# A graph network's edge loop: PE makes the next group's pair counts between its two sums, and DVE takes them at the start of the turn

## What is computed

```
def _prop_once(node_states, f_idx, t_idx, edge_features, w1, b1, w2, b2, w3, b3):
    from_states = node_states[f_idx]
    to_states = node_states[t_idx]
    edge_inputs = jnp.concatenate([from_states, to_states, edge_features], axis=1)
    edge_states = _mlp(edge_inputs, w1, b1, w2, b2, w3, b3)
    return jax.ops.segment_sum(edge_states, t_idx, num_segments=node_states.shape[0])
agg = _prop_once(node_states, from_idx, to_idx, edge_features, ...)
agg = agg + _prop_once(node_states, to_idx, from_idx, edge_features, ...)
...
S = jax.ops.segment_sum(X[src], dst, num_segments=n)     # second layer, three times
```

## Time and profile before

| | us |
|---|---|
| median of 3 runs | 2401.57 |
| lowest, highest | 2397.04, 2402.34 |
| the profiled execution, its own time | 2405.81 |
| its span, from the first to the last instruction | 2403.9 |
| first sum of the first turn, of the last turn | 67.0, 1907.8 |
| PE matmuls busy | 2278.5 (95%) |
| DVE busy | 1761.2 (73%) |
| ACT busy | 1230.7 (51%) |
| POOL busy | 1143.2 (48%) |

### The profile page before, as it was taken

One profiled execution on the slowest core, in us unless ns is written; L12 is line 12 of the kernel. 1 busy time (PEld: TensorE's weight loads), 2 busy tenths in 40 slices (PEclk: granted clock), 3 DMA queues, 4 the chain that ended last, 5 costly groups with the idle time before them and its releaser, 6 DMA issues. The chain is left out here.

```text
span 2403.9 us, 39417 instructions
## 1 busy us (share of the span) xinstructions
PE 2278.5 (95%) x12547; PEld 1876.2 (78%) x12547; DVE 1761.2 (73%) x4056; ACT 1230.7 (51%) x2106; POOL 1143.2 (48%) x846
## 2 busy tenths in 40 slices
PE   4999999999999999999999999999999879799997
PEld 3888888888888888888888888888888645588886
DVE  7888888888888888888888888888887557602114
ACT  4556556656656656556666566565665413211112
POOL 2556555656566666566566565665665300000000
PEclk9999999999999999999999999999999979899998
DMA  4356556446555445555535555544555450395873
GB/s 161 80 106 131 98 94 109 87 80 110 98 94 111 90 78 109 95 97 108 96 77 106 94 110 97 94 95 87 103 103 94 59 218 1 118 385 229 337 286 142
DMA packets 232338, 292.57 MB, mean 122 GB/s; under 512 B 126016, under 2 KB 189862, under 8 KB 223800
## 3 DMA queue, kind: packets, MB, share of 16 engines
q1 hardware_dynamic: 158756, 237.04, 36.0%
q0 software_dynamic: 73216, 54.58, 16.9%
q10 hardware_dynamic: 272, 0.05, 0.0%
HBM read 218.51 MB, written 73.08 MB: 121 GB/s over the span
## 5 line engine op out<-in xcount | busy, mean ns | idle before, releaser
L470 POOL DMA_INDIRECT sums<-outb,target x416 | 671.1, 1613 | 625.0 <-ACT outb L640 421.6
L463 POOL DMA_INDIRECT xg<-in_x,gidx x416 | 467.4, 1123 | 158.8 <-issue 140.9
L1237 PEld LDWEIGHTS ebank<-w3t,h 128*128 128x128 f32 x3328 | 387.4, 192 | 8.3 <-issue 0.3
L1237 PE MATMUL ebank<-w3t,h 128*128 128x128 f32 x3328 | 388.2, 275 | 0.2 <-ACT h L622 0.2
L1225 PE MATMUL ebank<-h1h,w2h 128*128 128x512 f32 x832 | 365.0, 439 | 5.1 <-DVE h1l L849 3.3
L622 ACT ACTIVATE h<-ebank,b2c 128x512 f32<-128x512 f32 x416 | 286.6, 689 | 116.2 <-issue 81.9
L608 ACT ACTIVATE h1h<-hpre 128x512 fp32r<-128x512 f32 x416 | 257.9, 628 | 154.6 <-DVE hpre L845 115.7
L1225 PE MATMUL ebank<-h1h,w2l 128*128 128x512 f32 x832 | 328.9, 395 | 0.0
L1225 PE MATMUL ebank<-h1l,w2h 128*128 128x512 f32 x832 | 326.3, 392 | 0.0
L849 DVE SCALAR_TENSOR_TENSOR h1l<-hpre,h1h 128x512 fp32r<-128x512 f32 x416 | 270.9, 691 | 17.2 <-ACT h1h L608 13.6
L845 DVE TENSOR_TENSOR hpre<-pb,ebank 128x512 f32<-128x512 f32 x416 | 265.1, 677 | 2.3 <-PE ebank L1211 2.2
(11 more groups left out here) (266 smaller groups left out, 3800.6 us busy)
## 6 DMA issues: line engine op xcount, KB each, us to landing
ring<-adj SPq DMA_DIRECT2D x54, 1568.0 KB, 8.4
rowb<-along SPq DMA_DIRECT2D x104, 512.0 KB
adj<-band SPq DMA_DIRECT2D x25, 1500.0 KB
ef<-in_edge_attr SPq DMA_DIRECT2D x103, 256.0 KB
stay<-adj SPq DMA_DIRECT2D x6, 1568.0 KB, 14.4
xg<-in_x,gidx POOLq DMA_INDIRECT x416
sums<-outb,target POOLq DMA_INDIRECT x416
sums<-band SPq DMA_DIRECT2D x2, 1664.0 KB
```

The costliest lines, as they stand in the source:

```text
L463: pool.indirect_dma_start(out=to, out_offset=None, in_=a["x"], in_offset=bass.IndirectOffsetOnAxis(ap=ids, axis=0)).then_inc(s_x[par], 16)
L470: pool.indirect_dma_start(out=tables[k % 2], out_offset=bass.IndirectOffsetOnAxis(ap=target[par][:, 1, k:k + 1], axis=0), in_=outb[par][:, ...
L1237: last = nc.tensor.matmul(bank[6 + way][:, t * P:(t + 1) * P], h2[:, way, k, t * P:(t + 1) * P], w3t[:, k, :], start=not bias and k == 0, ...
```

## The change

On PE, `pairs_of(g)` is no longer made between `turn_sd(g + 1)` and `second(g, 1)`. `total(g)` now makes `pairs_of(g + 1)` between the first sum and the second. In it a wait is added, for all four `hpre` of that group (`s_hp`), since `bank[4]` and `bank[5]` are free only then. Group 0 has its pair counts where they were.

On DVE, from turn 1 on, `count_pairs(g, 0)` is the first thing in the turn, then comes `nodes(g + 1)`, then `count_pairs(g, 1)`, and only then `compare`, `places` and `sums`. `lower_parts` now follows `sums` directly. No instruction of the computation is added or taken away.

```
-                    if ahead:
-                        nodes(g + 1, 1 - par, early=early == 2)
-                        compare(g + 1, 1 - par, turns + par)
-                    places(g, par, early=early > 0)
-                    if ahead:
-                        sums(g + 1)
                     if begin:
+                        nodes(1, 1, early=True)
+                        compare(1, 1, 0)
+                        places(0, 0, early=True)
+                        sums(1)
                         pair_keys()
                         pair_hot(0)
                         lower_parts(1)
                         dve.wait_ge(s_band, 2)
                         dve.wait_ge(s_ztab, 2 * 16)
-                    if fresh is not None:
-                        dve.wait_ge(s_fresh, fresh)
-                    count_pairs(g, 0)
-                    count_pairs(g, 1)
+                        count_pairs(0, 0)
+                        count_pairs(0, 1)
+                    else:
+                        if fresh is not None:
+                            dve.wait_ge(s_fresh, fresh)
+                        count_pairs(g, 0)
+                        if ahead:
+                            nodes(g + 1, 1 - par)
+                        count_pairs(g, 1)
+                        if ahead:
+                            compare(g + 1, 1 - par, turns + par)
+                        places(g, par, early=early > 0)
+                        if ahead:
+                            sums(g + 1)
...
                 def pairs_of(g):
 
                     pe.wait_ge(s_ah, g + 1)
+                    pe.wait_ge(s_hp, g * 4 + 4)
...
-                def total(g, par):
+                def total(g, par, ahead):
...
                     last.then_inc(s_sum, 1)
+                    if ahead:
+                        pairs_of(g + 1)
                     pe.wait_ge(s_es, g * 2 + 2)
...
                     if begin:
                         pair_keys()
-                    else:
-                        pairs_of(g)
                     second(g, 1)
```

More of the change, by code:

```diff
@@ L1316, in turn @@
                     third(g)
-                    total(g, par)
+                    total(g, par, ahead)
                 def into_each():
```

## The result

The changed kernel takes 2518.02 us (median of 4 runs, 2516.35 to 2519.22) against 2400.62 us for the kernel before (4 runs): a ratio of 1.0483, 95% interval 1.0469 to 1.0497. It is 117 us slower. The prediction was 2511 us, in a range of 2470 to 2541.

What follows compares the result with a forecast made beforehand. PE, busy 95% of the span, was taken to bound the kernel, others close behind. Turns of 18.95 against 17.92 us add 105 us, wraps 5; 2401.6 + 110 gives about 2511 us, range 2470 to 2541.

Steps and rivals of the forecast that it cites:

- Pairs on PE: PE, between the two sums: the four pair matmuls cost 0.96 us, as in the old place; bounds 0.83 and 1.1.
- The second sum's wait: PE's second sum starts at t + 1.80, t being the first sum's start, so its wait for `es` is covered.
- The first count is hidden: DVE, start of turn: half 0's count ends at t + 2.95, before `into` at t + 2.99, hidden by 0.04 us.
- The bubble: DVE, between `into` and second `outdeg`: 0.36 us idle for the slot read; chain to `sd` 1.05 us later in all.
- From `same` to the fourth block: DVE to ACT to PE: 3.05 us to `sd`, 2.40 to the fourth block at t + 9.84; PE waits 1.37 us.
- The rest of the turn: PE, behind the fourth block: 1.45 us to L1211, at t + 11.29, then 7.66 to the next first sum; 18.95 us.
- The sum: Edge loop: 1.03 us more in turns 1 to 102 is 105 us, with the wraps' 5, 110; about 2511.
- A: Rival: PE's fourth block doesn't wait, the turn is 17.54 us and some wraps, 24 to 30 us less, 2375; chance 0.06.

Runs made afterwards that it cites:

- e8: The kernel before with DVE's `pair_hot` moved behind `ways`; ratio 0.9920 to the kernel before.
- e10: e8 with DVE's target, the add that waits for the table's DMAs, also moved behind `sdl`; ratio 0.9908 to the kernel before.
- e3: The changed kernel with only DVE's second count moved back behind `sd`; 2409.67 us against 2409.09 for the kernel before, ratio 1.0008.
- e2: The changed kernel with ACT writing `h` of the second block ahead of `sdh`; ratio 1.0248 to the kernel before.
- e11: e3 with DVE's target, the add that waits for the table's DMAs, moved behind `sdl`; ratio 0.9916 to the kernel before.
- e1: The changed kernel with DVE's old order, both counts behind `sd`, and PE's new order kept; ratio 1.0206 to the kernel before.
- e5: e3 with ACT also writing `h` of the second block ahead of `sdh`; ratio 1.0033 to the kernel before.
- e4: The changed kernel with the slot of half 1 read ahead of the first count; ratio 1.0353 to the kernel before.
- e6: The kernel before with only ACT's swap, `h` of the second block written ahead of `sdh`; ratio 0.9987 to the kernel before.

## Why the prediction was right, by its own steps

1. **Pairs on PE.** Taken at 0.96 us in both places. In the new place the second sum starts 0.85 behind the first pair (865.34 to 866.19), which is what the forecast's own rows give for its lower bound: 1.02 less 0.38, over three, four times, is 0.85, not 0.83. Counted to the next block they add less: the first block is at t + 2.50 in the middle, where it is at 1.75 in e8 and e10, so 0.75 us; the forecast was 2.71. In the old place their removal gave back 0.77: from the first to the third block it took 5.27 us (the medians of two parts, 3.34 and 1.93) and takes 4.50 now. So both terms were some 0.2 too large, and the second doesn't reach the turn, as PE waits behind it.
2. **The second sum's wait** is covered, as said: 0.4 us in all.
3. **The first count is hidden.** `outdeg` at t + 2.09 for 2.18, since the first pair starts 0.84 behind the first sum and not 0.94. `into` at 2.78 for 2.99; it doesn't wait for the count, and follows the first block by 0.28 as in the earlier trace rows.
4. **The bubble.** Counted as the forecast does, from `into` to `outdeg` less 0.34, it is 0.82 - 0.34 = 0.48 us for 0.36 (the row's idle, from the end of `into`, is 0.39): `into` came 0.2 earlier and the second count only 0.1. The two errors partly cancel, with `same` at 4.29 for 4.39.
5. **From `same` to the fourth block.** 3.04 and 2.40 us, as read from the earlier trace rows. This was the step that the sign hung on. e3 shows it by undoing its cause, e2 by cutting its link. PE's wait for `h` is 118.9 us in all, 1.17 a turn, where 1.37 and some 140 in all were forecast.
6. **The rest of the turn.** 1.49 for 1.45, then 7.67 for 7.66 (875.72 to 883.39). The turn in the middle is 18.94 for 18.95. That it agrees to a hundredth is luck: the 0.1 too little at `same` is made good by nearly as much too much behind it.
7. **The sum.** 19.02 in the mean where the sum with wraps said 19.00; 102 turns of 1.10 more make the 112 us. The measured difference of medians is 117, the forecast was 110; the 5 us between 112 and 117 are no part of the loop's sum, as the profiled execution of before (2405.81) was that much slower than its median (2400.62).

Of the rivals, A (the gain that filling PE's gap promises) failed where the prediction said: filling the gap is worth nothing when the engine next behind has less slack than what is put ahead of it. In e11 its turn does come out, once DVE has that slack, and in e10 without the change's order. The Trainium skill (Perfetto Trace Analysis, section "Optimization Strategy") would have us find the gaps of the most contended engine and make what blocks it start sooner or complete faster. The prediction took A for what that rule gives, and that was a wrong reading: the change makes nothing start sooner, it puts other work into the gap. The change that does what the rule says is e8, where the second `es` starts 0.20 us behind the first sum's start in nearly all turns, and it is 0.8% faster: the measurement agrees with the rule there. The Trainium skill's other figure, a floor of about 600 ns for a tensor_load (DMA: Bandwidth & Descriptors, section "Latency and other measured facts"), isn't borne out: the load's median is 306 ns (the prediction read 302) and it is 306 in the changed kernel too, and the idle of the bubble is 0.39 us.

The expectations were worse than the prediction, mostly at one place: I followed the chain only to L1211 and took the 7.65 us behind it as fixed. In e1, e2 and e5 it grew to between 7.8 and 7.9; as the timelines read, moving PE forward against DVE used up the slack of `hpre` and the first `es`, which is ready 0.14 to 0.23 us ahead of the sum there and 0.57 in the changed kernel. e3 missed by its late turns, and e4 by the delay of its first count.

## What to carry to other kernels

Before work is moved to fill a gap of the busiest engine, read what the engines next to it have left at the points where it waits for them, and look for a turn in which they were late by chance: one late turn of the kernel before gave the term that the sign of the change hung on (2.40 us from `sd` to PE). A step is best placed by what waits behind it: the same second count costs 4.8% ahead of `sd` and nothing behind it, but with the first count behind `sd` too it is 2% (e1). And a gap of the busiest engine isn't by itself the time that can be won: the same gap was filled (the changed kernel, 4.8% slower; e3, nothing) and made to go by moving ACT's work (e6, 0.1% faster) or DVE's (e8, 0.8% faster). What decided was what became of the rest of the turn.

## What the runs showed of the hardware that was not expected

The copy to the second `es` depends only on PE's third layer, yet it starts at two distinct times. In the kernel before it starts 0.20 us behind the start of the first sum, or earlier, in 52 of 102 turns, and 0.55 to 0.85 us behind in 45. It is within 0.3 us in 99 of 102 turns of the changed kernel, in 96 of e6, 97 of e8 and all of e10.

How long before the first sum the first `es` was ready doesn't decide it. With 0.3 to 0.5 us to spare, 42 of 68 turns of the kernel before are late (0.5 us or more); with 0.1 to 0.3, 3 of its 28, 46 of 71 in e1 and 4 of 94 in e6; with 0.5 or more, 1 of 91 in the changed kernel, 11 of 93 in e3 and 17 of 93 in e4. ACT's two copies to `es` in two turns of the kernel before, whose first sums start at 1179.65 and at 1197.19, and in one of e6, whose first sum starts at 1191.34:

```profile
1178.63 0.57 ACT L630 COPY es<-ebank 128x512 f32<-128x512 f32 x1
1179.85 0.59 ACT L630 COPY es<-ebank 128x512 f32<-128x512 f32 x1 [0.66 <-PE ebank L1237]
```

```profile
1196.16 0.57 ACT L630 COPY es<-ebank 128x512 f32<-128x512 f32 x1
1197.85 0.59 ACT L630 COPY es<-ebank 128x512 f32<-128x512 f32 x1 [1.12 <-PE ebank L1237]
```

```profile
1190.54 0.57 ACT L630 COPY es<-ebank 128x512 f32<-128x512 f32 x1
1191.54 0.58 ACT L630 COPY es<-ebank 128x512 f32<-128x512 f32 x1 [0.43 <-PE ebank L1236]
```

In the first two the first `es` is ready 0.45 and 0.46 us ahead of the sum, and only the second copy of the second turn is late; in e6 it is ready 0.23 ahead, and the second copy is on time. So PE can lose some 0.48 us at the second sum (1.32 us behind the first for 0.84) with no wait at the first. e6 and e8 each remove it, by moves on two different engines. Why the signal of a finished matmul is late in those turns isn't settled: whether PE's signals are held while its queue waits, or its last matmuls end later than the modelled ends say, these runs don't tell.

A set of four bf16 matmuls with 500 columns puts the next f32 matmul 0.85 us behind its start between the two short sums, moves the block after that by 0.75, and gave back 0.77 us where it was taken out from between long ones; before, I had read 0.96 for that place from start distances.
